# Cross-attention of a decoder layer: values and totals of a head group run in the first quarter of the group after next, with a second buffer for the first head's exponentials

## What is computed

```python
q = (x @ Wq).reshape(B, N, HEADS, hd).transpose(0, 2, 1, 3)
k = (context @ Wk).reshape(B, M, HEADS, hd).transpose(0, 2, 1, 3)
v = (context @ Wv).reshape(B, M, HEADS, hd).transpose(0, 2, 1, 3)
scores = jnp.einsum('bhid,bhjd->bhij', q, k) * scale
scores = jnp.where(context_mask[:, None, None, :], scores, max_neg)
attn = jax.nn.softmax(scores, axis=-1)
out = jnp.einsum('bhij,bhjd->bhid', attn, v)
return out.transpose(0, 2, 1, 3).reshape(B, N, DIM) @ Wo
```

## Time and profile before

| | |
|---|---|
| median of 3 runs | 3772.2 us (3767.72 to 3776.98) |
| the profiled execution | 3775.88 us, span of its instructions 3774.1 us |
| PE, PEld busy | 3639.7 us (96%), 3139.7 us (83%) |
| DVE, ACT, POOL busy | 2361.0 us (63%), 1731.9 us (46%), 1305.9 us (35%) |
| mean granted PE clock | 0.982 |
| `scores` L1180, `shifted` L1192, `values` L1205 | 1024, 1536, 3072 PE instructions |

### The profile page before, as it was taken

How to read it: one execution, slowest core, us unless ns; L and a number is a source line. 1 busy time by engine, 2 the same in 40 slices (tenths; PEclk the granted TensorE clock), 3 DMA queues, 4 the chain that set the end, 5 groups by cost and what they waited for, 6 DMA issues and landing times. The chain is left out here.

```text
span 3774.1 us, 84215 instructions
## 1 busy us (share of the span) xinstructions
PE 3639.7 (96%) x28244; PEld 3139.7 (83%) x28244; DVE 2361.0 (63%) x5543; ACT 1731.9 (46%) x4278; POOL 1305.9 (35%) x1388
## 2 busy tenths in 40 slices
PE   8999999999979999999999999849999999999999
PEld 7888888888868888888888888638998899989998
DVE  6888888888846666666666666576433434434343
ACT  4555555555435555555555555413333333333332
POOL 2333333333325656666556566510101101011010
PEclk9999999999989999999999999869999999999999
DMA  4222222222243434444434343223324334234232
GB/s 127 60 54 63 54 63 53 64 53 64 72 122 94 112 106 104 108 116 107 121 96 113 104 108 97 71 68 94 121 82 122 107 98 123 82 118 123 85 108 69
DMA packets 315057, 349.72 MB, mean 93 GB/s; under 512 B 45308, under 2 KB 232036, under 8 KB 314884
## 3 DMA queue, kind: packets, MB, share of 16 engines
q1 hardware_dynamic: 305796, 318.26, 30.7%
q0 software_dynamic: 9088, 29.17, 2.4%
HBM read 183.23 MB, written 38.91 MB: 59 GB/s over the span
## 5 line engine op out<-in xcount | busy, mean ns | idle before, releaser
L1627 DVE TENSOR_REDUCE x_mx<-x_psS 112x1 f32<-112x752 f32 x512 | 479.7, 937 | 382.2 <-PE x_psS L1180 378.6
L2423 DVE TENSOR_TENSOR hid<-e_psU,act_g 128x280 f32<-128x280 f32 x256 | 115.1, 450 | 622.6 <-PE e_psU L34 585.8
L1462 ACT ACTIVATE x_pt<-x_psE 125x448 f32<-125x448 f32 x768 | 389.6, 542 | 227.6 <-PE x_psE L1192 217.7
L1051 POOL TENSOR_TENSOR part<-x_pt 125x448 f32<-125x448 f32 x255 | 292.4, 1147 | 506.0 <-ACT x_pt L1462 497.1
L2049 POOL DMA_INDIRECT out<-ex_y,sidx x40 | 39.8, 995 | 1020.4 <-DVE ex_y L2457 1010.2
L635 POOL TENSOR_TENSOR qks<-qks,cos 128x448 f32<-128x448 f32 x128 | 148.1, 1157 | 657.0 <-DMA qks<-qk 657.0
L1180 PE MATMUL x_psS<-k_st,q_st 97*112 97x376 f32 x1024 | 287.9, 362 | 24.1 <-DMA k_st<-mk 16.3
L32 PE MATMUL e_psG<-ex_hi,g_hi 128*128 128x280 f32 x1024 | 304.2, 297 | 6.7 <-ACT act_g L2208 4.5
L32 PE MATMUL pj<-xT_hi,win_hi 128*128 128x224 f32 x1024 | 302.2, 295 | 4.0 <-PEq L185 3.9
L2208 ACT ACTIVATE act_g<-e_psG 128x280 f32<-128x280 f32 x256 | 103.7, 405 | 426.4 <-PE e_psG L34 412.1
L1053 POOL TENSOR_TENSOR part<-part,x_pt 125x448 f32<-125x448 f32 x255 | 292.3, 1146 | 20.0
(11 more groups left out here) (305 smaller groups left out, 10890.3 us busy)
## 6 DMA issues: line engine op xcount, KB each, us to landing
k_st<-kT SPq DMA_DIRECT2D x768, 93.8 KB, 2.2
raw_g<-in_L_ffn_wg SPq DMA_DIRECT2D x128, 256.0 KB
raw_u<-in_L_ffn_wu SPq DMA_DIRECT2D x128, 256.0 KB
raw_d<-in_L_ffn_wd SPq DMA_DIRECT2D x128, 256.0 KB
qks<-qk SPq DMA_DIRECT2D x512, 56.0 KB, 2.0
q_st<-qT SPq DMA_DIRECT2D x384, 56.0 KB, 2.0
ctxt<-in_ctx SPq DMA_DIRECT2D x16, 1125.0 KB
xt<-in_x SPq DMA_DIRECT2D x16, 448.0 KB, 3.7
```

Of the source, the lines that this page charges most:

```text
L1051: pool.tensor_tensor(part[:], pt[j][:, 0, :], pt[j][:, 1, :], ALU.add).then_inc(parted, 1)
L1462: act.activation(pt[j][:, i, :], psE[(j + i) % 2][0:KR, 0:2 * T], ACT.Exp, scale=XD ** -0.5).then_inc(exp_done, 1)
L1627: dve.tensor_reduce(mx[:, j, h:h + 1], psS[0:HT, :, 0:376], AX.XY, ALU.max).then_inc(s_taken, 1)
L2423: dve.tensor_tensor(h[ring][:, halves[s]], psU[:, 0:CH], act_g[i][:, halves[s]], ALU.mult).then_inc(S["mul"], 1)
```

## The change

1. `values(n - 2)` now stands in the second gap of quarter 0 of group `n`, with `totals(n - 2)` directly behind it. The calls at the end of the group before and in quarter 1 are gone.
2. The exponentials of head 0 have two buffers, since those of block `n - 1` are written before PE has read those of block `n - 2`. The block sums have two buffers for head 0 and one for the others; for head 1 POOL waits for the totals of the block before.
3. Room for that comes from `qT`, cut from four column blocks to two (`i % 2`), with ACT's waits on `q_placed` to match.

```diff
-            qT = [sb(c, f"qT{i}", [P, KD, T], F32R) for i in range(2)]
+            qT = [sb(c, f"qT{i}", [P, 2, T], F32R) for i in range(2)]
...
-            pt = [op.pt[0], sb(c, "x_pt1", [KR, 3, 2 * T]), op.pt[2], op.pt[3]]
+            pt_first = [op.pt[0], sb(c, "x_pt0_odd", [KR, 3, 2 * T])]
+            pt_other = [sb(c, "x_pt1", [KR, 3, 2 * T]), op.pt[2], op.pt[3]]
...
-            ptsum = [sb(c, f"ptsum{i}", [KR, T]) for i in range(8)]
+            sum_first = [sb(c, f"ptsum0_{i}", [KR, T]) for i in range(2)]
+            sum_other = [sb(c, f"ptsum{i}", [KR, T]) for i in range(1, 4)]
...
                             if j == 0 and not below(t, 2):
                                 hold(pool, gate, z_full, t - 1)
+                            elif j == 1 and not below(t, 1):
+                                hold(pool, gate, z_full, t)
...
                             if j == 0:
+                                if pprev:
+                                    values(n - 2, (g + 2) % 4)
+                                    totals(n - 2, g)
                                 if g == 0:
                                     project_v(U("V04"), 0, 4)
...
                             elif j == 1:
-                                if pprev:
-                                    totals(n - 2, g)
...
                                 elif g == 3:
                                     done(U("V15"))
-                                values(n - 1, gp)
...
                     turn_max(last("M1_4"), n - 1, 1)
+                    values(n - 2, 2)
                     totals(n - 2, 2)
...
-                        if i in (0, 2) and not below(b, 1):
-                            act.wait_ge(q_placed[i // 2], 192 * b)
+                        if i == 0 and not below(b, 1):
+                            act.wait_ge(q_placed[1], 192 * b)
+                        elif i == 2:
+                            act.wait_ge(q_placed[0], 192 * b + 192)
```

More of the change, by code:

```diff
@@ L918, in placed, with pt, ptsum @@
                 return 224 * b + (64, 128, 176, 224)[g]
+            def pt(g, j):
+                return pt_other[j - 1] if j else pt_first[g % 2]
+            def ptsum(g, j):
+                return sum_other[j - 1] if j else sum_first[g % 2]
             def all_batches(e, body):
@@ L990, in place_q @@
                                 sp.dma_start(q_st[32 * s:32 * s + 32, 8 * half + j:8 * half + 8:4, :].bitcast(F32),
-                                             qT[p][rows, 2 * half:2 * half + 2, :].bitcast(F32)).then_inc(q_placed[half], 16)
+                                             qT[p][rows, :, :].bitcast(F32)).then_inc(q_placed[half], 16)
                     load_x(1, unit_of(-1, "X1"))
@@ L1048, in sum_blocks @@
                         for j in heads:
-                            n, out = 4 * t + j, ptsum[4 * (g % 2) + j]
+                            n, out, p = 4 * t + j, ptsum(g, j), pt(g, j)
                             pool.wait_ge(exp_done, 3 * n + 3)
-                            pool.tensor_tensor(part[:], pt[j][:, 0, :], pt[j][:, 1, :], ALU.add).then_inc(parted, 1)
+                            pool.tensor_tensor(part[:], p[:, 0, :], p[:, 1, :], ALU.add).then_inc(parted, 1)
                             pool.wait_ge(parted, 2 * n + 1)
-                            pool.tensor_tensor(part[:], part[:], pt[j][:, 2, :], ALU.add).then_inc(parted, 1)
+                            pool.tensor_tensor(part[:], part[:], p[:, 2, :], ALU.add).then_inc(parted, 1)
                             if j == 0 and not below(t, 2):
                                 hold(pool, gate, z_full, t - 1)
+                            elif j == 1 and not below(t, 1):
+                                hold(pool, gate, z_full, t)
                             pool.wait_ge(parted, 2 * n + 2)
@@ L1205, in values @@
                                 m = pe.matmul(psY[32 * j:32 * j + 32, 0:T], v[:, r, head * XD:(head + 1) * XD],
-                                              pt[j][:, r // 2, (r % 2) * T:(r % 2 + 1) * T], start=(r == 0), stop=(r == KB - 1))
+                                              pt(g, j)[:, r // 2, (r % 2) * T:(r % 2 + 1) * T], start=(r == 0), stop=(r == KB - 1))
                         m.then_inc(y_full, 1)
@@ L1216, in totals @@
                         for j in range(4):
-                            m = pe.matmul(psZ[32 * j:32 * j + 32, 0:T], ones[:], ptsum[4 * (g % 2) + j][:], start=True, stop=True)
+                            m = pe.matmul(psZ[32 * j:32 * j + 32, 0:T], ones[:], ptsum(g, j)[:], start=True, stop=True)
                         m.then_inc(z_full, 1)
@@ L1394, in high_q @@
                             act.wait_ge(valid_done, b + 1)
-                        if i in (0, 2) and not below(b, 1):
-                            act.wait_ge(q_placed[i // 2], 192 * b)
+                        if i == 0 and not below(b, 1):
+                            act.wait_ge(q_placed[1], 192 * b)
+                        elif i == 2:
+                            act.wait_ge(q_placed[0], 192 * b + 192)
                         o = full(u)
-                        act.activation(qT[0][:, i, :], o[:, 0:T], ACT.Copy, scale=valid[:, 0:1]).then_inc(hi_done, 1)
+                        act.activation(qT[0][:, i % 2, :], o[:, 0:T], ACT.Copy, scale=valid[:, 0:1]).then_inc(hi_done, 1)
                     def high_k(u, b, g, s):
@@ L1453, in out_logits, with exps @@
                         act.activation(dst, o[0:HT, 0:2 * E].rearrange("p (h e) -> p h e", h=2), ACT.Copy).then_inc(pj_free[u.bank], 1)
-                    def exps(t, j, units):
+                    def exps(t, g, j, units):
                         n = 4 * t + j
@@ L1461, in exps @@
                             act.wait_ge(st_full, 3 * n + i + 1)
-                            act.activation(pt[j][:, i, :], psE[(j + i) % 2][0:KR, 0:2 * T], ACT.Exp,
+                            act.activation(pt(g, j)[:, i, :], psE[(j + i) % 2][0:KR, 0:2 * T], ACT.Exp,
                                            scale=XD ** -0.5).then_inc(exp_done, 1)
@@ L1568, in body @@
                                 if prev:
-                                    exps(n - 1, j, range(3) if j == 3 else (0, 1))
+                                    exps(n - 1, (g + 3) % 4, j, range(3) if j == 3 else (0, 1))
                                 first_gap(g, j)
                                 if prev and j < 3:
-                                    exps(n - 1, j, (2,))
+                                    exps(n - 1, (g + 3) % 4, j, (2,))
                                 second_gap(g, j)
@@ L1576, in _ @@
                     n = 4 * B
-                    exps(n - 1, 0, range(3))
+                    exps(n - 1, 3, 0, range(3))
                     high_max(unit_of(B - 1, "M1_4"), 3, 1)
                     for j in range(1, 4):
-                        exps(n - 1, j, range(3))
+                        exps(n - 1, 3, j, range(3))
                     for h in range(2):
@@ L1614, in low_q @@
                         hi_ready(b, f"Q{i}")
-                        dve.scalar_tensor_tensor(qT[1][:, i, :], pj[u.bank][:, 0:T], valid[:, 0:1], qT[0][:, i, :].bitcast(F32),
+                        dve.scalar_tensor_tensor(qT[1][:, i % 2, :], pj[u.bank][:, 0:T], valid[:, 0:1], qT[0][:, i % 2, :].bitcast(F32),
                                                  ALU.mult, ALU.subtract).then_inc(pj_free[u.bank], 1)
@@ L1791, in _ @@
                     dve.wait_ge(exp_done, 3 * 4 * n)
-                    dve.tensor_reduce(ptsum[7][:], pt[3][:].rearrange("p a (s t) -> p t (a s)", s=2), AX.X, ALU.add).then_inc(last_sum, 1)
+                    dve.tensor_reduce(ptsum(3, 3)[:], pt(3, 3)[:].rearrange("p a (s t) -> p t (a s)", s=2), AX.X, ALU.add).then_inc(last_sum, 1)
                     for i in range(2):
```

## The result

The changed kernel takes 3911.33 us (median of 5 runs, 3909.58 to 3912.26) against 3775.75 us in the runs beside it: 1.0364 times the time of before, 95% interval 1.0349 to 1.0378. It is slower by 136 us. Forecast were 97 us more, 3869 us, and a range that ended at 3897.

The account below looks back on a forecast made before the run. PE was taken to bound the cross-attention. 66.7 us of moved work and waits plus 30 of clock falls made +97: 3873 from the profiled 3775.88, stated as 3869 us against the median of three runs; range 3826 to 3897.

Parts of the forecast that it names:

- The bound and the chain: Cross-attention: PE sets the time; at the ends of g = 3 and g = 0 `values` covers PE's wait for DVE's last maximum.
- The sum without the clock: Cross-attention, 139.5 added in quarter 0, less 70.1 at group ends and 2.7 of bank wait: 66.7 us longer.
- Removed from quarter 1: 0.72: Quarter 1 of each group: taking the totals away saves PE 0.72 us, their instructions and the way in and out.
- The clock: Emptied ends of g = 3 and g = 0: 20 of 30 idle times bring a clock fall, 1.5 us each, 30 us.
- The upper bound of 51: Emptied group ends: the most the clock falls would cost, all idle times followed by a fall, in full, 51 us.
- The third rival: Emptied ends: every idle time brings a fall, or falls last for two such stretches; 3890 to 3901 us, chance 0.13.
- 11 for the keys: DMAs placing the next group's keys: their visible waits could grow by up to 0.7 in 16 batches, +11 us.
- POOL 0: Quarter 0 and head 1: totals needing the fourth head's sum earlier, and POOL's new wait for totals, cost 0.
- `q_placed` 0: ACT's second waits on `q_placed`: for DMAs PE has already waited for to start the group, so 0.
- The keys: DMAs placing the next group's keys: visible waits of 3.5 us could go or grow; taken as 0.
- 2.97 of the forecast: Quarter 0: time inserted per group by values and totals, 2.41 + 0.40 + 0.16 with about half a way in.
- 3.13: Quarter 0: upper bound in us of the inserted time per group, with all of the way in paid again.

## Why the prediction was wrong

*The bound and the chain:* right. The maximum stands where it stood behind `shifted`, PE waits for it at the ends of g = 3 and g = 0, 2.88 between the two `scores` (2.9 forecast), 82.9 us of waits (80 forecast) in 62 places (50). Both kernels with another order in the chain (the maximum ahead of `low_max`, `high_max` ahead of the third exponential) moved it by the step taken off it.

*The sum without the clock:* 66.7 forecast. The kernel with filled ends has 88.16 us per batch against 83.25, 4.91 more; times 15.5 batches that is 76, an estimate. By group, measured against forecast: g = 0 + 2.16 (2.19), g = 1 - 0.14 (- 0.16), g = 2 + 0.90 (0.34), g = 3 + 1.99 (2.25). So the size was right in three of four. In g = 2 the step "Removed from quarter 1: 0.72" counted a gain that was none: with the totals gone, V14 comes to a bank that DVE frees no earlier, and waits 0.7 for the residual. The same totals had been a cover there, which the prediction checked at the ends of the groups and not in quarter 1. That is 10 of the missing 39 us. With the residual half a quarter earlier the wait is gone and g = 2 is at 23.79, level with before, where 0.34 more was forecast for the group.

*The clock:* this is the step that failed: "two in three are followed by a fall, 20 of 30", 1.5 us each, 30 us. There were falls at 29 of the 30 ends, 150 us together, and every second one lasted 6.8 us and not 3.4. The upper bound of 51 held falls of 3.4 only, and the range was built on it. Measured by filling the ends, the clock costs 4.0 us per batch, about 60 in all and not 30. With 76 that is the 136. The share of two in three came from two idle times, one of 1.86 us with a fall and one of 1.54 without. The trace of before also held a fall in its last batch, behind an idle time of PE of 1.12 us, which the prediction did not use:

```profile
2400.68:2401.81 1.13, 0.01 (x1) 0.03 (x1) 1.10 (x3) 0.24 (x1) 0.74 (x1) 1.00 0.68 165
2402.90:2406.30 3.40, 3.39 (x28) 1.89 (x29) 1.61 (x4) 2.03 (x4) 2.62 (x4) 0.50 0.55 128
```

The third rival named "falls last for two such stretches", but its price held the same 51 as one stretch for each wait, beside 11 for the keys, whose waits did not come. So its 3890 to 3901 was too low as well: the clock took 60, and the residual's 10 were not in it. Why a fall takes 6.8 us at one end and 3.4 at the other, and in some kernels does not come, is open.

*The rest:* POOL 0 and `q_placed` 0 were right: the kernel with the buffers alone is as fast as before, and PE waits for neither in the changed kernel. The keys were put at 0; their waits of 3.5 us went, as the prediction allowed. The pair behind each other costs 1783.94 - 1780.72 = 3.22 from `scores` to the turn behind it in g = 2 of the changed kernel:

```profile
1780.72 0.51 PE L1190 MATMUL x_psS<-k_st,q_st 97*112 97x376 f32 x2
1781.15 2.48 PE L1215 MATMUL x_psYZ<-x_pt,x_v 125*32 125x224 f32 x48
1783.45 0.56 PE L1227 MATMUL x_psYZ<-ptsum,x_ones 125*32 125x224 f32 x8
1783.94 0.60 PE L1180 MATMUL x_pj<-ident,x_mx 112*128 112x112 f32 x4
```

Less 0.34 for `scores` to a turn without it (1721.58 to 1721.92 in the kernel before) that is 2.88, 0.09 below the 2.97 of the forecast. So putting the two blocks together does save time, as the change intends, but little: 3.13 - 2.88 = 0.25 by this reading and 0.14 by the group of g = 1, an estimated 9 to 15 us in 62 groups, against 136 us net the other way. The Trainium skill's "TensorEngine Tiling (Array Packing)", section "Key Properties", says that changing the tiling mode drains the engine. The trace agrees in direction, with these 0.14 to 0.25 us for one change of mode less per group.

## What to carry to other kernels

Before a block is moved off a place, look for the wait that it covers there, at both places it leaves: a bound engine with no visible waits may be filling them with work. A wait that is made visible can have a second price, the clock, and here that one did not follow the number of waits: measure it by filling the wait with matmuls of the same length whose result nobody reads. Keep such a filler short where it stands in a hardware loop: with 192 instructions more per pass the jumps back cost 35 us here, with 24 more 9.

## What was not expected of the hardware

- Falls of the granted clock repeated in every batch at the same places, and batch lengths held: 92.2 us in the changed kernel and, in most batches, also with 0.86 us more work, 88.8 us with 0.95 less, where the same work without falls takes 88.16 or an estimated 87.2. Both lengths are close to whole multiples of the shortest fall in the record, 27 and 26 times. That is a relation of the numbers only; that batches and falls keep step is seen, and its cause was not tested.
- Falls came behind idle times of only 1.0 us (with the maximum ahead of `low_max`), while one of 1.54 us in the experts and 13 of 2.22 us in the kernel with the earlier residual left the clock alone.
- A hardware loop whose PE program grew by 192 matmuls and weight loads per pass waited about 3 us at each of its 12 jumps back, with 217 instruction packets and not 106; with 24 more it waited 3 times (133 packets). The cause was not isolated.
